# An embedding by groups of four tiles, and result tables filled later, in a small transformer tower

## What is computed

```python
h = layer_norm(emb_word[input_ids] + emb_pos[:S][None], emb_ln_s, emb_ln_b)
for l in range(L):                                   # L = 4
    q = heads(h @ Wq[l] + bq[l])
    k = heads(h @ Wk[l] + bk[l])
    v = heads(h @ Wv[l] + bv[l])
    a = band_attention(q, k, v, mask)
    ...
    h = layer_norm(h + a @ Wo[l] + bo[l], ln1_s[l], ln1_b[l])
    f = jax.nn.gelu(h @ W1[l] + b1[l], approximate=False)
    h = layer_norm(h + f @ W2[l] + b2[l], ln2_s[l], ln2_b[l])
```

## Time and profile before

| what | us |
|---|---|
| median of 3 runs | 1865.72 |
| lowest and highest | 1864.42, 1872.34 |
| span of the profiled execution, first to last instruction | 1874.5 |
| PE busy | 1483.1 (79%) |
| DVE busy | 1247.8 (67%) |
| ACT busy | 977.2 (52%) |
| POOL busy | 808.0 (43%) |
| mean granted clock of PE | 0.895 of full |

### The profile page before, as it was taken

How to read it: one execution, slowest core, us unless ns; L and a number is a source line. 1 busy time by engine, 2 the same in 40 slices (tenths; PEclk the granted TensorE clock), 3 DMA queues, 4 the chain that set the end, 5 groups by cost and what they waited for, 6 DMA issues and landing times.

```text
span 1874.5 us, 42615 instructions
## 1 busy us (share of the span) xinstructions
PE 1483.1 (79%) x13098; PEld 1235.0 (66%) x13098; DVE 1247.8 (67%) x3542; ACT 977.2 (52%) x2392; POOL 808.0 (43%) x1177
## 2 busy tenths in 40 slices
PE   0589889798897997998988759759668887499992
PEld 0367678677676776776767648449646766389992
DVE  4788966788767888668896652433379896434344
ACT  0378733688434885348873223225348882155550
POOL 6577333684235762247733310124356521144440
PEclk9899989899899997999998968669869996599996
DMA  4666101743005550035610000147534511257765
GB/s 105 176 149 127 36 1 33 170 86 84 1 5 138 108 121 2 1 70 140 128 33 1 1 14 1 45 138 224 173 89 100 112 22 45 97 175 237 225 212 179
DMA packets 144317, 178.26 MB, mean 95 GB/s; under 512 B 22096, under 2 KB 106128, under 8 KB 143952
## 3 DMA queue, kind: packets, MB, share of 16 engines
q1 hardware_dynamic: 136784, 158.18, 32.9%
q0 software_dynamic: 7296, 17.18, 2.8%
HBM read 132.96 MB, written 42.34 MB: 94 GB/s over the span
## 4 chain that ended last, share of the span: by engine, by line
PE 31%; DVE 14%; issue 4%; DMA 2%; ACT 2%; POOL 2%; SPq 0%; DVEq 0%; POOLq 0%; ACTq 0%
PE bank L1473 7%; DVE ptl L799 4%; PE bank L1459 2%; DVE neg_max L792 2%; PE bank L645 1%; DVE xn L912 1%; PE bank L563 1%; PE bank L1460 1%; PE bank L1463 1%; PE bank L1461 1%; PE bank L1462 1%; PE bank L1217 1%; DMA xn<-y_rows 1%; PE bank L431 1%; PE bank L584 1%
## 5 line engine op out<-in xcount | busy, mean ns | idle before, releaser
L685 ACT ACTIVATE prob<-bank,neg_max 128x192 f32<-128x192 f32 (+1 forms) x960 | 406.9, 437 | 109.3 <-DVE neg_max L792 97.0
L792 DVE TENSOR_REDUCE neg_max<-bank 128x2 f32<-128x384 f32 (+1 forms) x480 | 274.3, 572 | 99.0 <-PE bank L544 91.4
L799 DVE TENSOR_TENSOR ptl<-bank,pth 128x384 f16<-128x384 f32 (+1 forms) x480 | 275.5, 574 | 4.6 <-ACT pth L698 4.0
L563 PE MATMUL bank<-ident,prob 128*128 128x128 f32 x1536 | 268.4, 288 | 0.0
L698 ACT ACTIVATE pth<-bank 128x384 f16<-128x384 f32 (+1 forms) x480 | 244.3, 509 | 9.3 <-PE bank L563 9.2
L652 ACT ACTIVATE xx<-bank 128x256 fp32r<-128x256 f32 x256 | 95.5, 386 | 196.0 <-PE bank L431 192.0
L544 PE MATMUL bank<-kx,qx 96*128 96x192 bf16 (+1 forms) x960 | 168.1, 257 | 1.1 <-DVE xx L766 1.1
L563 PEld LDWEIGHTS bank<-ident,prob 128*128 128x128 f32 x1536 | 162.9, 143 | 0.1
L584 PE MATMUL bank<-v,pth 128*128 128x33 bf16 x1152 | 138.4, 180 | 21.2 <-DVE ptl L799 18.0
L645 PE MATMUL bank<-w,fbuf 128*128 128x192 f32 x768 | 140.7, 327 | 2.0 <-DVE h L889 2.0
L734 ACT ACTIVATE fbuf<-bank,b 128x512 f32<-128x512 f32 x96 | 65.8, 687 | 146.5 <-PE bank L453 146.4
(11 more groups left out here) (295 smaller groups left out, 4522.5 us busy)
## 6 DMA issues: line engine op xcount, KB each, us to landing
xn<-in_e_seg SPq DMA_DIRECT2D x34, 768.0 KB
w<-in_e_w SPq DMA_DIRECT2D x23, 576.0 KB
qk_rows<-fbuf SPq DMA_DIRECT2D x128, 96.0 KB, 2.3
qx<-qk_rows SPq DMA_DIRECT2D x35, 288.0 KB, 4.0
kx<-qk_rows SPq DMA_DIRECT2D x35, 288.0 KB, 5.8
qk_rows<-w SPq DMA_DIRECT2D x80, 96.0 KB, 2.3
qx<-qk_rows SPq DMA_DIRECT2D x35, 192.0 KB, 4.6
kx<-qk_rows SPq DMA_DIRECT2D x35, 192.0 KB, 5.2
```

Source lines behind the costliest of these rows:

```text
L563: last = nc.tensor.transpose(bank[BT[p % 2]][:, c * P:c * P + P], probs_at(p, banded, c * P, P), ident[:, :])
L685: nc.scalar.activation(probs_at(p, banded, qt * n, n), scores_at(p, n)[:, qt, :], ACT.Exp, bias=neg_max[:, b % 2, hd, qt:qt + 1], scale=1. ...
L792: nc.vector.tensor_reduce(neg_max[:, b % 2, hd, :], scores_at(p, D if banded else S), AX.X, ALU.max, negate=True).then_inc(max_ready.sem, 1)
L799: nc.vector.tensor_tensor(ptl[:, p % 2, 0:n], bank[BT[p % 2]][:, 0:n], pth[:, p % 3, 0:n], ALU.subtract)\
```

## The change

The token numbers are loaded first, then the place rows and the norm's rows (with a semaphore of their own, `place_in`, into `vf`, where the window goes too), the first weights, and only then the constants and the mask. The gathers are counted by groups of four tiles: groups 0 and 1 are gathered, then POOL does the power of group 0 and the low parts of the first weights (ACT now makes the high parts), gathers group 2, does group 1's power, gathers group 3, and does the remaining powers and sums in between; the clearing of `middle` comes after the first sums. DVE adds the place rows with one instruction for a group, takes its statistics, and norms it when its turn comes: tiles 0 to 3 of the opening follow norm 0 and the mask, then come norm 1 and group 2's sums, the three chunks, group 3's sums and norm 2, and the rest of the opening. The mask is made in one pass over the keys and two minimum operations for all sequences. PE's and ACT's parts of the opening keep their order. The eight fills of `y_rows` are issued after the fourth layer's work of SP.

```diff
@@ -200,6 +200,7 @@
+        place_rows, window = vf[:, 0:2, :], vf[:, 2:4, :]
...
+        key_mask = probs[:, 0:B * S].rearrange("p (b n) -> p b n", b=B)
...
@@ -1624,19 +1628,20 @@

         @block.sync
         def _(sp):
-            for dst, src in ((ident, "ident"), (lo_rows, "lo_rows"), (q_scale, "q_scale"),
-                             (neg_in, "neg_in"), (pad_keys, "pad_keys")):
-                sp.dma_start(dst[:, :], a[src]).then_inc(const_in.sem, 16)
+            sp.dma_start(tok[:, :], a["x"]).then_inc(tok_in.sem, 16)
+            sp.dma_start(place_rows, a["L0_tok_emb_pos"]).then_inc(place_in.sem, 16)
             for k, src in enumerate(("L0_tok_emb_ln_s", "L0_tok_emb_ln_b")):
                 dst = (ln_s, ln_b)[k]
-                sp.dma_start(dst[:, 1, :], a[src].unsqueeze(0).to_broadcast([P, D])).then_inc(const_in.sem, 16)
-
-            sp.dma_start(hb[:, 0:2, :], a["L0_tok_emb_pos"]).then_inc(const_in.sem, 16)
-            sp.dma_start(tok[:, :], a["x"]).then_inc(tok_in.sem, 16)
-
+                sp.dma_start(dst[:, 1, :], a[src].unsqueeze(0).to_broadcast([P, D])).then_inc(place_in.sem, 16)
+            sp.dma_start(raw[:, :, 0:QKV], a["seg_a"][0, :, :, :]).then_inc(rows_x.sem, 16)
+            sp.dma_start(bqk[:, :], a["bqk"][0, :, :]).then_inc(rows_x.sem, 16)
+            for dst, src in ((ident, "ident"), (lo_rows, "lo_rows"), (q_scale, "q_scale"), (neg_in, "neg_in"), (pad_keys, "pad_keys")):
+                sp.dma_start(dst[:, :], a[src]).then_inc(const_in.sem, 16)
             sp.dma_start(xn[:, 0:8, :].bitcast(I32), a["mask_BS_i1_0"].unsqueeze(0).to_broadcast([P, B, S]))\
                 .then_inc(mask_in.sem, 16)
-            sp.dma_start(hb[:, 4:6, :], a["window"]).then_inc(mask_in.sem, 16)
+            sp.dma_start(window, a["window"]).then_inc(mask_in.sem, 16)
+            sp.dma_start(row_bv[:, :], a["bv"][0, :, :].to_broadcast([P, D])).then_inc(rows_x.sem, 16)
+            sp.dma_start(row_bo[:, :], a["bo"][0, :, :].to_broadcast([P, D])).then_inc(rows_bo.sem, 16)
...
@@ -1647,14 +1652,6 @@
                     qk_read()
                 sp.dma_start(bqk[:, :], a["bqk"][it, :, :]).then_inc(rows_x.sem, 16)

-            load_x(0)
-            sp.dma_start(row_bo[:, :], a["bo"][0, :, :].to_broadcast([P, D])).then_inc(rows_bo.sem, 16)
-            sp.wait_ge(mask_ok.sem, 1)
-            filler = flat(mask[:, :, :], "p t d -> p (t d)").bitcast(F32).rearrange("p (t d) -> p t d", d=D)
-            for s in range(2):
-                for i in range(4):
-                    sp.dma_start(y_rows[s][8 * P * i:8 * P * (i + 1), :].rearrange("(t p) d -> p t d", p=P), filler)\
-                        .then_inc(filled.sem, 16)
             def sp_layer(it):
                 sp_heads(sp, it, 0, True)
                 sp.wait_ge(y_read.sem, y_read.at(it, 0))
@@ -1679,6 +1676,11 @@
             with sp.Fori(0, L - 1) as it:
                 sp_layer(it)
             sp_layer(L - 1)
+            filler = flat(mask[:, :, :], "p t d -> p (t d)").bitcast(F32).rearrange("p (t d) -> p t d", d=D)
+            for s in range(2):
+                for i in range(4):
+                    sp.dma_start(y_rows[s][8 * P * i:8 * P * (i + 1), :].rearrange("(t p) d -> p t d", p=P), filler)\
+                        .then_inc(filled.sem, 16)
             sp.wait_ge(wa_ready.sem, wa_ready.at(L, 1))

             sp.wait_ge(h_ready.sem, h_ready.at(L, 0))
@@ -1727,29 +1729,45 @@
             ch = Chain(ctx, nc, pool, "pool_order", alone)
             for s in (att_ready, v3_ready, xc_pow_ready, seg_q_ready):
                 s.start(pool)
-            for b in range(2):
-                ch.link(nc.gpsimd.memset(middle[b], 0.0))
             nc.gpsimd.memset(neg_half[:, :], -0.5).then_inc(zeroed.sem, 1)
             pool.wait_ge(zeroed.sem, 1)
             pool.wait_ge(tok_ok.sem, 1)
-            for t in range(NT):
-                pool.indirect_dma_start(out=h[:, t, 0:D], out_offset=None, in_=a["L0_tok_emb_word"],
-                                        in_offset=bass.IndirectOffsetOnAxis(ap=toku[:, t:t + 1], axis=0))\
-                    .then_inc(gathered.sem, 16)
+
+            def first_rows(g):
+                for t in range(GT * g, GT * g + GT):
+                    pool.indirect_dma_start(out=h[:, t, 0:D], out_offset=None, in_=a["L0_tok_emb_word"],
+                                            in_offset=bass.IndirectOffsetOnAxis(ap=toku[:, t:t + 1], axis=0))\
+                        .then_inc(gathered[g].sem, 16)
+
+            def first_sums(g):
+                if g < 2:
+                    pool.sem_inc(hb_ready.sem, (12, 4)[g])
+                pool_hb(pool, 0, normed(2, GT * g) - 2 * NT, g, row_bo)
+
+            first_rows(0)
+            first_rows(1)
+            pool_rstd(pool, ch, 0, 1 - NG, 0, 1e-12)
+            pool.wait_ge(first_high.sem, 2)
             pool.wait_ge(rows_x.sem, 48)
-            pool.wait_ge(const_in.sem, 16 * 8)
+            pool.wait_ge(const_in.sem, 16 * 5)
             ch.mark(nc.gpsimd.tensor_tensor(bqk[:, :], bqk[:, :], q_scale[:, :].to_broadcast([P, 3]), ALU.mult))
-            pool_weights(ch, wa, QKV).then_inc(wa_ready.sem, 1)
+            nc.gpsimd.tensor_tensor(wa[1][:, 0:QKV], raw[:, 0, 0:QKV], wa[0][:, 0:QKV].bitcast(F32), ALU.subtract)
+            ch.done(ch.n)
+            nc.gpsimd.tensor_tensor(wa[3][0:D2, 0:QKV], raw[0:D2, 1, 0:QKV], wa[2][0:D2, 0:QKV].bitcast(F32), ALU.subtract)\
+                .then_inc(wa_ready.sem, 1)
+            first_rows(2)
+            pool_rstd(pool, ch, 0, 2 - NG, 1, 1e-12)
+            first_rows(3)
             pool.wait_ge(rows_bo.sem, 16)
-            for g in range(NG + 1):
-                if g < NG:
-                    pool_rstd(pool, ch, 0, g + 1 - NG, g, 1e-12)
-                if 1 <= g < NG:
-                    if g == 1:
-                        pool.wait_ge(mask_ok.sem, 1)
-                    if g < 3:
-                        pool.sem_inc(hb_ready.sem, (12, 4)[g - 1])
-                    pool_hb(pool, 0, normed(2, GT * (g - 1)) - 2 * NT, g - 1, row_bo)
+            first_sums(0)
+            for b in range(2):
+                if b == 0:
+                    pool.wait_ge(mask_ok.sem, 1)
+                ch.link(nc.gpsimd.memset(middle[b], 0.0))
+            pool_rstd(pool, ch, 0, 3 - NG, 2, 1e-12)
+            first_sums(1)
+            pool_rstd(pool, ch, 0, 4 - NG, 3, 1e-12)
+            first_sums(2)
             pool_ones(ch)
@@ -1844,7 +1862,10 @@
         def _(act):
             for s in (xh_ready, qf_ready, exp_done, pad_ready, hi_ready, f_ready, xc_qk_ready, xc_v_ready, xc_e_ready, xc_y_ready, r_ready, g2_exp):
                 s.start(act)
-            act.wait_ge(const_in.sem, 16 * 8)
+            act.wait_ge(rows_x.sem, 48)
+            for i in range(2):
+                nc.scalar.activation(wa[2 * i][:, 0:QKV], raw[:, i, 0:QKV], ACT.Copy).then_inc(first_high.sem, 1)
+            act.wait_ge(const_in.sem, 16 * 5)
@@ -1915,8 +1936,6 @@
                       xc_pt_ready, xc_o_ready, g2_max, sum_ready):
                 s.start(dve)

-            nc.vector.memset(wa[3][D2:P, :].bitcast(F32), 0.0)
-            nc.vector.memset(wb[3][D2:P, :].bitcast(F32), 0.0).then_inc(padded.sem, 1)
             dve.wait_ge(tok_in.sem, 16)
             ch.link(nc.vector.tensor_copy(tokf[:, 0, :], tok[:, :]))
             ch.link(nc.vector.tensor_scalar(tokf[:, 1, :], tokf[:, 0, :], 0.0, float(VOCAB), ALU.is_lt, ALU.mult))
@@ -1924,30 +1943,33 @@
             ch.link(nc.vector.tensor_scalar(tokf[:, 1, :], tokf[:, 0, :], 0.0, float(VOCAB - 1), ALU.max, ALU.min))
             nc.vector.tensor_copy(toku[:, :], tokf[:, 1, :]).then_inc(tok_ok.sem, 1)
+            nc.vector.memset(wa[3][D2:P, :].bitcast(F32), 0.0)
+            nc.vector.memset(wb[3][D2:P, :].bitcast(F32), 0.0).then_inc(padded.sem, 1)
+
+            def first_add(g):
+                dve.wait_ge(gathered[g].sem, 16 * GT)
+                rows = h[:, GT * g:GT * g + GT, 0:D].rearrange("p (b q) d -> p b q d", q=2)
+                ch.link(nc.vector.tensor_tensor(rows, rows, place_rows.unsqueeze(1).to_broadcast([P, 2, 2, D]), ALU.add))
+                dve_stats(dve, ch, 0, 0, g, None)
+
+            def first_norm(g):
+                if g < 2:
+                    dve.sem_inc(h_ready.sem, (12, 4)[g])
+                dve_affine(dve, ch, 0, g + 1 - NG, g, 1)
+
+            dve.wait_ge(place_in.sem, 48)
+            first_add(0)
             dve.wait_ge(mask_in.sem, 32)
-            km = xn[:, 8:16, :]
-            ch.link(nc.vector.tensor_copy(km, xn[:, 0:8, :].bitcast(I32)))
-            ch.link(nc.vector.tensor_scalar(xn[:, 0:8, :], km, 0.0, -1.0, ALU.is_gt, ALU.add))
-            ch.link(nc.vector.tensor_scalar(km, xn[:, 0:8, :], -NEG_IN, None, ALU.mult))
-            for t in range(NT):
-                qt = t % 2
-                last = nc.vector.tensor_tensor(mask[:, t, :], hb[:, 4 + qt, :],
```

(35 more changed lines are left out.)

4 lines of the change are left out of this document (3 added, 1 removed).

## The result

The changed kernel takes 1857.35 us (median of 15 runs, 1848.15 to 1865.77), the kernel before 1867.75 (15 runs, 1857.46 to 1874.84). The ratio is 0.9942, with a 95% interval of 0.9925 to 0.9958: 10.4 us faster. The forecast was 1844.6, and the time lies outside its range of 1839 to 1855.

What follows compares the result with a forecast made beforehand. The prediction took DVE to bound the opening, everything else waiting for it from 37.44 to 80.77 us. Terms -24.7, -1.8, +4.8, -4.1, +0.6, +2.1, +2.0 sum to -21.1, off 1865.7: 1844.6, range 1839 to 1855.

Steps and rivals of the forecast that it cites:

- The start: Opening: token load first in SP's queue, so DVE adds the first group at 12.7 instead of 37.44 us; -24.7.
- The mask: Opening: mask making moves from DVE's idle time onto the path, after the first rows are there; +4.8 us.
- The adds: Opening: four DVE adds of 3.9 us in all replace sixteen that took 5.71; -1.8 us.
- The chunk wait: Opening: DVE's 4.14 us wait before the first pieces goes, as the first tiles are split before the second norm; -4.1.
- Waits for group 1 and for POOL's rstds: Opening: DVE waits for the second four gathers, +2.1 us, and for rstds queued behind gathers on POOL, +2.0.
- starved as feared: Rival in the opening: DVE slows POOL's gathers to 2.43 us each, gain only 12.4, time 1853.3; chance 0.25.
- The second wait: Opening: the wait for values and tiles 4 to 7 stays as it was; no term in the sum.
- the handovers: Opening: extra waits between adds, statistics and single groups, some 0.15 to 0.2 us each, a few times; +0.6.
- The Trainium skill's rule of the shared port: Opening: VectorE and GpSimd lock one port pair, so gathers 9 to 16 could be blocked; trace said to agree in part.
- Is the lead kept?: After the opening: nothing waits on an absolute time, so the 21.1 us gained stays to the end.
- the granted clock of PE falling at a worse moment: Layer 3's end: with the fills, part of the rival that the lead is given back, time 1865.1; chance 0.09.
- The fills: Eight result-table fills, moved after SP's last issue of layer 3, take about 20.5 us under cover; cost 0.

Runs made afterwards that it cites:

- loads_late: Changed kernel with the mask, window and output bias loads held until the first four gathers land, key mask made after the first norm; 1854.54 us, ratio 0.9921.
- late: Changed kernel with 20 clearings of a scratch tile on POOL in front of the first gather; 1877.99 us, ratio 1.0052 to the kernel before.

## Why the prediction was wrong

**Where the 12.8 us between 1844.6 and 1857.35 come from.** The first score came less early than said, 17.4 for 21.1: 3.7. The lead lost 7.0 behind it. And the median that the terms were taken off, 1865.7 from three runs, was 1867.75 in fifteen: 2.0. With the lead of 17.4 kept whole the time would have been 1850, inside the range.

**The forecast of the first score was near, in part by luck.** It said -21.1, to 59.7; the two profiles differ by 18.4, to 62.37, and the means of the traces by 17.4. From the first add to the first score it said 3.6 us more than before and 3.4 came, but out of other terms.

- The start: -24.7 was said, -21.8 came. The first gather was earlier than taken (4.44 for 5.2) and the pace the quiet one, so four were issued by 9.34 (9.9). But the landing was taken as 2.84, from gathers that had the DMA engines nearly to themselves. It was 6.3. The text named this as what could go wrong, a group that shares the engines with the mask load, and gave it no price in the range.
- The mask: +4.8 said, 1.19 and 3.41 measured, 4.6.
- The adds: four now take 0.96, 0.96, 0.95 and 1.34, 4.2 in place of 5.71: -1.5 for -1.8. The last has 0.4 us beside POOL's sums in it.
- The chunk wait is gone as said, and the first chunk stood at 33.79 ("near 32").
- Waits for group 1 and for POOL's rstds: 2.1 and 2.0 said, 1.03 and 0.59 measured. The gathers were not starved as feared: one of sixteen took 4.60 and one 2.13, the third group took 8.6 in all and the fourth 6.3, and nearly all of it had cover.
- What had no term: DVE held up by POOL, 1.1 us in the norm's four and 3.1 in the cast, together 4.2. The prediction asked only what DVE does to POOL's gathers.
- Nor had the same delay in the kernel before, which the change takes away. There six steps of the norms took 0.67 or 0.68 in place of 0.34, each beside one of POOL's sums, while now all take 0.34 or 0.35: -2.0. DVE and POOL before:

```profile
48.78 0.68 DVE L941 SCALAR_TENSOR_TENSOR h<-hb,rstd,ln_b 128x128 f32<-128x128 f32 x1
...
48.68 0.63 POOL L993 TENSOR_TENSOR hb<-h,row_bo 128x192 f32<-128x192 f32 x1 [0.37 <-DVE h L941]
```

- The second wait, for values from PE, didn't just stay: 1.21 and 0.71 in place of 0.63 and 0.32, +1.0. The wait of 0.35 for the first rstd and the 0.17 for a second chunk are gone, and some 0.1 is left for the handovers, taken at 0.6.
- Together these make -18.4, the measured difference of the two profiles (-21.8, +4.6, -1.5, -4.1, +1.6, +4.2, -2.0, +1.0, -0.5, +0.1).

**The Trainium skill's rule of the shared port.** The cast of 3.50 us beside POOL's two-input sums is such a case the other way round. The page "SBUF — State Buffer", section "Who interferes with whom", says that casts can enter a mode that takes both port pairs, that the pair is an exclusive lock, and that issue order decides who blocks. By that rule the victim may be either engine. The traces agree: 3.50 for 0.43 for the cast that came 0.03 us after POOL's sums began, and in loads_late 0.69 for the one that came into their midst, with the sums long instead. The long case lasts as long as a row of POOL's instructions, though, not one of them, each of the four sums being some 0.55. The prediction had only set the rule against the gathers; of the eight that it meant, the 4.60 stands beside the two minimum operations, and in loads_late two gathers beside the same operations took 1.32 and 1.36. So for gathers the traces agree in part, as it said.

**The step that failed is "Is the lead kept?"** It said that nothing behind the opening waits on an absolute time, so the lead is kept in full. The premise holds: **late** moved the start by 19.8 and the time by 21.1. The conclusion doesn't: 7 us of 17.4 are missing (5.7 by the means), and at the later start of **late** again 7. Nothing waits on an absolute time, and yet the same text of the layers ran longer behind another opening, a cost that the prediction put at nothing. The text gave "the granted clock of PE falling at a worse moment" a share of 0.09 together with the fills, and a price of all or nothing. The fills are cleared by two runs. The clock is shown to be worth 8 us in the gate stage, in single traces of one program (gate stretch 169.2 and 161.2) and between kernels: of the seven changed kernels without added transposes four stayed at 0.50 (168.3 to 169.2) and three rose (160.2 to 161.2), while both such traces of the opening of before rose (160.0 and 162.4). But both kernels gain when it is held at 1.00, and how much more the changed one loses there, 3 us by medians and 1.5 by means, is not told apart from the spread. The layers hold 3 us, by ten traces against four, and 2.4 of them are DVE's longer standstill at the three turns of the loop, which is in every trace of the one kind and in none of the other.

What isn't settled: whether the changed program misses the rise more often at all (nine traces are few), and what makes DVE stand longer where its loop turns; the fourth packet of instructions is a sign and no proof. An experiment for it would pad or shorten DVE's opening alone, in either kernel.

A tempting shortcut misleads here. The mean granted clock of all runs is 0.894 for the kernel before and 0.888 for the changed one, and it would seem to explain everything. But the opening itself counts in that mean: its windows show a clock of 0.97 over 80.77 us before, where PE mostly idles, and 0.86 over 62.37 after. With the same clock for all the rest, (0.894 x 1868 - 0.97 x 80.77) / 1787 = 0.891, the changed kernel's mean would be (0.86 x 62.37 + 0.891 x 1788) / 1850 = 0.890. Only 0.002 of the 0.006 is left for the stages behind, with means that are rounded to 0.001.

**The fills.** Cost 0 was right, within the 3 us that the runs can tell. SP issues them from 925.71 in the changed kernel.
